# Between the two parts of a fused 8-sequence block: weights of the first local layer loaded into used-up weight memory, statistics taken per batch

## The reference

```python
x = x + L0_attn(layernorm(x), ...)           # piece "a"
x = x + L0_xattn(layernorm(x), ctx, ctx)     # "b", an mLSTM cell
x = x + L0_ffn(layernorm(x), ...)            # "c", 8 experts for each of 4 heads, and an MLP
x = x + L1_attn(layernorm(x), ...)           # "d"
x = x + L1_xattn(layernorm(x), ctx, mask)    # "e"
x = x + L1_ffn(layernorm(x), ...)            # six local layers:
    for i in range(6):
        x = attn_layer(shift_tokens(x), Wqkv[i], q_scale[i], k_scale[i], Wo[i]) + x
        x = ffn_layer(shift_tokens(x), ln_g[i], ln_b[i], W1[i], b1[i], W2[i], b2[i]) + x
```

## Time and profile before

| | us |
|---|---|
| median of 3 runs | 4306.43 |
| lowest and highest | 4299.49, 4312.36 |
| the profiled execution: its own time | 4305.56 |
| the profiled execution: span | 4303.6 |

### The profile page before, as it was taken

How to read it: one execution, slowest core, us unless ns; L and a number is a source line. 1 busy time by engine, 2 the same in 40 slices (tenths; PEclk the granted TensorE clock), 3 DMA queues, 4 the chain that set the end, 5 groups by cost and what they waited for, 6 DMA issues and landing times. The chain is left out here.

```text
span 4303.6 us, 81290 instructions
## 1 busy us (share of the span) xinstructions
PE 3902.0 (91%) x25848; PEld 2840.7 (66%) x25848; DVE 2894.1 (67%) x9138; ACT 2278.2 (53%) x6540; POOL 2268.3 (53%) x2084
## 2 busy tenths in 40 slices
PE   7789989887578999999999999999999999999995
PEld 5667777666346666666666666666666666666664
DVE  4576777655367777767767677766776777777762
ACT  2333333332156666656666666665666566666651
POOL 1565555556175555546556555555655655555540
PEclk8899999988799999999999999999999999999998
DMA  3775565667200000100100001010010001010000
GB/s 116 158 165 139 134 135 135 131 146 158 71 6 11 11 29 19 32 19 9 42 21 27 12 11 38 20 32 9 9 42 18 30 11 41 17 31 11 8 4 25
DMA packets 137427, 224.20 MB, mean 52 GB/s; under 512 B 24656, under 2 KB 98320, under 8 KB 135440
## 3 DMA queue, kind: packets, MB, share of 16 engines
q0 software_dynamic: 40960, 134.25, 14.1%
q1 hardware_dynamic: 96016, 84.41, 6.2%
HBM read 191.39 MB, written 2.10 MB: 45 GB/s over the span
## 5 line engine op out<-in xcount | busy, mean ns | idle before, releaser
L1549 PE MATMUL pj<-l_w_qkv,l_xT 128*128 128x512 f32 x2304 | 1074.1, 603 | 18.6 <-issue 12.6
L1494 POOL TENSOR_TENSOR l_qk_rot<-l_qk_cos,l_qk_sin 128x512 f32<-128x512 f32 x384 | 558.0, 1453 | 411.0 <-DVE l_qk_sin L1814 364.4
L364 POOL DMA_INDIRECT f_rows<-in_emb,f_expert x512 | 514.1, 1004 | 414.1 <-DVE f_expert L1009 227.2
L1549 PEld LDWEIGHTS pj<-l_w_qkv,l_xT 128*128 128x128 f32 x2304 | 418.5, 194 | 404.9 <-issue 389.8
L1629 PE MATMUL pj<-l_xnT,l_w 128*128 128x256 f32 x2112 | 518.8, 391 | 117.9 <-DVE l_hT L1857 108.6
L1709 ACT ACTIVATE l_probs<-l_probs,l_low 128x128 f32<-128x128 f32 x1536 | 593.8, 390 | 2.5 <-DVE l_low L1832 0.7
L1475 POOL TENSOR_TENSOR l_rstd<-l_var_eps,l_minus_half 128x2 f32<-128x2 f32 x48 | 33.4, 696 | 941.8 <-DVE l_var_eps L1788 941.8
L1629 PEld LDWEIGHTS pj<-l_xnT,l_w 128*128 128x128 f32 x2112 | 384.1, 191 | 192.9 <-DVE l_hT L1857 120.0
L1806 DVE TENSOR_REDUCE l_ss<-l_qk_sq 128x8 f32<-128x512 f32 x384 | 261.5, 681 | 366.9 <-ACT l_qk_sq L1696 201.9
L1675 ACT ACTIVATE l_qk_raw<-pj 128x512 f32<-128x512 f32 x384 | 227.3, 592 | 464.7 <-PE pj L1549 450.5
L1832 DVE CUSTOM_DVE_ANT_0 l_probs<-sc,l_shut,l_r_q 128x128 f32<-128x128 f32 x1536 | 437.4, 345 | 51.8 <-PE tp L1588 43.1
(11 more groups left out here) (312 smaller groups left out, 7415.9 us busy)
## 6 DMA issues: line engine op xcount, KB each, us to landing
l_w_qkv<-in_L_ffn_Wqkv SPq DMA_DIRECT2D x12, 1024.0 KB, 6.1
l_w<-in_ff_w SPq DMA_DIRECT2D x6, 1408.0 KB, 6.9
f_rows<-in_emb,f_expert POOLq DMA_INDIRECT x512, 5.8
l_w_qkv<-in_L_ffn_Wqkv SPq DMA_DIRECT2D x12, 512.0 KB, 4.7
l_xs<-l_stream SPq DMA_DIRECT2D x48, 128.0 KB
l_w_o<-in_L_ffn_Wo SPq DMA_DIRECT2D x6, 1024.0 KB, 5.4
l_xf<-l_stream SPq DMA_DIRECT2D x48, 128.0 KB
l_xs<-l_stream SPq DMA_DIRECT2D x48, 127.0 KB
```

Source lines behind the costliest of these rows:

```text
L364: pool.indirect_dma_start(rows[:, j % RH, k, :], None, dram["emb"], bass.IndirectOffsetOnAxis(ap=expert[:, n % 2, at:at + 1], axis=0)).the ...
L1494: pool.tensor_tensor(qk_rot[:, i % ROTS, :], qk_cos[:, b, :], qk_sin[:, b, :], ALU.add).then_inc(rotated if s == 0 else pool_front, 1)
L1549: last = pe.matmul(pj[b][:, :], xT[:, k, t * P:(t + 1) * P], w_qkv[:, k, s * INNER + c * 512:s * INNER + (c + 1) * 512], start=(k == 0), s ...
```

## The change

- `w_qkv` and `w_o` are allocated outside both parts (class `Shared`). In the first part the same memory holds `a_w` (in `w_o`) and `c_wg`, `c_wu`, `c_wd` (in `w_qkv`).
- SyncE, at the end of its order in the first part, waits until `a_y` of the last batch is done and issues the load of `w_o` for layer 0, then waits for the last readers of the three MLP weights and issues those of `w_qkv`. The loads are gone from the start of the second part; `qk_gain` is loaded there as before.
- VectorE takes the entry statistics of a batch (`f_stats`) behind its `e_u`, and POOL the power (`f_rstd`) at the end of its next step. The 16-tile statistics and POOL's power go from the second part.
- VectorE scales one batch at a time, and `entry_done` counts batches. SyncE's `stage_attn` for a batch of layer 0 waits for that batch only.

In `ORDER`, `("f_stats", -5)` is added to "vector" right behind `("e_u", -5)`, ahead of `("c_coef2", -3)`, and `("f_rstd", -6)` to "gpsimd" at the end of its step. The core of the rest:

```diff
-        a_w = sb("a_w", [P, 4, KC, D])
+        a_w = shared.w_o[:, :, :].rearrange("p (w k) d -> p w k d", w=4)
...
-        c_wg, c_wu = sb("c_wg", [P, KC, INTER]), sb("c_wu", [P, KC, INTER])
-        c_wd = sb("c_wd", [P, MC, D])
+        ffn = shared.w_qkv[:, :, :].rearrange("p k n -> p (k n)")
+        c_wg, c_wu = (ffn[:, i * KC * INTER:(i + 1) * KC * INTER].rearrange("p (k n) -> p k n", k=KC) for i in range(2))
+        c_wd = ffn[:, 2 * KC * INTER:2 * KC * INTER + MC * D].rearrange("p (c d) -> p c d", c=MC)
...
+            sp.wait_ge(ps_full, Slot("a_y", BATCH - 1).full)
+            shared.load_o(sp, 0)
+            sp.wait_ge(ps_full, max(Slot(f"c_m{i}", BATCH - 1).full for i in range(MC)))
+            sp.wait_ge(m_used[0], BATCH)
+            sp.wait_ge(m_used[1], BATCH)
+            shared.load_qk(sp, 0)
+            shared.load_v(sp, 0)
...
+            def f_rstd(n):
+                pool.wait_ge(measured, n + 1)
+                pool.tensor_tensor(shared.rstd[:, n, :], shared.var_eps[:, n, :], minus_half[:, 0:TILES], ALU.pow).then_inc(shared.entry_ready, 1)
+
+            do["f_rstd"] = f_rstd
...
+            def f_stats(n):
+                s = Slot("e_u", n)
+                dve.wait_ge(s.taken, s.after)
+                for t in range(TILES):
+                    last = V.bn_stats(f_bn[:, t, :], xall[:, n, t, :])
+                chain.link(last)
+                for t in range(TILES):
+                    last = V.bn_aggr(shared.mv[:, n, t, :], f_bn[:, t, :])
+                chain.link(last)
+                V.tensor_scalar(shared.var_eps[:, n, :], shared.mv[:, n, :, 1], 1e-5, None, ALU.add).then_inc(measured, 1)
+
+            do["f_stats"] = f_stats
...
             def stage_attn(n, row, first):
-                if not first:
+                if first:
+                    sp.wait_ge(entry_done, row + 1)
+                    apart(sp, passed)
+                else:
                     sp.wait_ge(res_f, n - BATCH + 1)
                     apart(sp, passed)
...
-            load_qk(0)
-            load_v(0)
+            load_gain(0)
             sp.wait_ge(consts_set, 2)
-            sp.wait_ge(entry_done, 1)
             stage_attn(0, 0, True)
-            load_o(0)
             load_1(0)
             load_cols(0)
             load_2(0)
...
-                pool.wait_ge(pool_init, 1)
-                pool.wait_ge(entry_stats, 1)
-                pool.tensor_tensor(all_rstd[:, :], all_var[:, :], all_half[:, :], ALU.pow).then_inc(entry_rstd, 1)
...
-                tiles_in = xall[:, :, :, :].rearrange("p b t d -> p (b t) d")
-                tiles_out = stream[:, :, :, :].rearrange("p b t d -> p (b t) d")
-                for i in range(ALLT):
-                    last = nc.vector.bn_stats(all_bn[:, i, :], tiles_in[:, i, :])
-                last.then_inc(dve_entry, 1)
-                dve.wait_ge(dve_entry, 1)
-                for i in range(ALLT):
-                    last = nc.vector.bn_aggr(all_mv[:, i, :], all_bn[:, i, :])
-                last.then_inc(dve_entry, 1)
-                dve.wait_ge(dve_entry, 2)
-                nc.vector.tensor_scalar(all_var[:, :], all_mv[:, :, 1], 1e-5, None, ALU.add).then_inc(entry_stats, 1)
-                dve.wait_ge(entry_rstd, 1)
-                for i in range(ALLT):
-                    last = nc.vector.tensor_scalar(tiles_out[:, i, :], tiles_in[:, i, :], all_mv[:, i, 0:1], all_rstd[:, i:i + 1],
-                                                   ALU.subtract, ALU.mult)
-                last.then_inc(entry_done, 1)
-                dve.wait_ge(entry_done, 1)
+                for row in range(BATCH):
+                    dve.wait_ge(shared.entry_ready, row + 1)
+                    for t in range(TILES):
+                        last = nc.vector.tensor_scalar(stream[:, row, t, :], xall[:, row, t, :], shared.mv[:, row, t, 0:1], shared.rstd[:, row, t:t + 1],
+                                                       ALU.subtract, ALU.mult)
+                    last.then_inc(entry_done, 1)
+                dve.wait_ge(entry_done, BATCH)
...
+    def load_qk(self, sp, l):
+        n = self.w_qkv.shape[2] // 3
+        for k in range(KC):
+            sp.dma_start(self.w_qkv[:, k, 0:2 * n], self.dram["L1_ffn_Wqkv"][l, k * P:(k + 1) * P, 0:2 * n]).then_inc(self.wqk_loaded, 16)
+
+    def load_v(self, sp, l):
+        n = self.w_qkv.shape[2] // 3
+        for k in range(KC):
+            sp.dma_start(self.w_qkv[:, k, 2 * n:3 * n], self.dram["L1_ffn_Wqkv"][l, k * P:(k + 1) * P, 2 * n:3 * n]).then_inc(self.wv_loaded, 16)
+
+    def load_o(self, sp, l):
+        sp.dma_start(self.w_o[:, :, :], self.dram["L1_ffn_Wo"][l].rearrange("(c p) n -> p c n", p=P)).then_inc(self.wo_loaded, 16)
...
+        shared = Shared(w_qkv=sb("w_qkv", [P, KC, 3 * inner]), w_o=sb("w_o", [P, inner // P, D]), mv=sb("entry_mv", [P, BATCH, TILES, 2]),
+                        var_eps=sb("entry_var_eps", [P, BATCH, TILES]), rstd=sb("entry_rstd", [P, BATCH, TILES]),
+                        wqk_loaded=ctx.enter_context(nc.semaphore("wqk_loaded")), wv_loaded=ctx.enter_context(nc.semaphore("wv_loaded")),
+                        wo_loaded=ctx.enter_context(nc.semaphore("wo_loaded")), entry_ready=ctx.enter_context(nc.semaphore("entry_ready")), dram=dram)
```

More of the change, by code:

```diff
@@ L8 @@
 from contextlib import ExitStack
+from dataclasses import dataclass
 import concourse.bass as bass
@@ L39, in apart, with first_layers @@
     eng.sem_inc(passed, 1)
-def first_layers(nc, xall, x_loaded, ident, ident_bf, dram):
+def first_layers(nc, xall, x_loaded, ident, ident_bf, shared, dram):
     H4, DH = 4, 64
@@ L93, in first_layers @@
         ("c_gather5", -4), ("c_gather6", -4), ("c_gather7", -4), ("c_gather8", -4), ("c_gather9", -4), ("c_gather10", -4), ("e_rstd", -5),
+        ("f_rstd", -6),
     ]
@@ L1141, in _, with local_layers @@
             dve.wait_ge(s.taken, s.after)
-def local_layers(nc, xall, ident, ident_bf, passed, dram, layers, out_dram):
+def local_layers(nc, xall, ident, ident_bf, passed, shared, dram, layers, out_dram):
     H, DH = 16, 64
@@ L1211, in sem @@
             return ctx.enter_context(nc.semaphore("l_" + name))
-        w_qkv = sb("w_qkv", [P, KC, 3 * INNER])
-        w_o = sb("w_o", [P, INNER // P, D])
+        w_qkv, w_o = shared.w_qkv, shared.w_o
         w_1 = sb("w_1", [P, KC, TAIL + P])
@@ L1385, in layer @@
                         apart(sp, passed)
-                        load_v(l + 1)
+                        shared.load_v(sp, l + 1)
                     if r == 2 and not first:
@@ L1877, in _, with sb @@
                 nc.vector.tensor_tensor(xall[:, row, :, :], xall[:, row, :, :], stream[:, row, :, :], ALU.add).then_inc(summed, 1)
+@dataclass
+class Shared:
+    w_qkv: object
+    w_o: object
+    mv: object
+    var_eps: object
+    rstd: object
+    wqk_loaded: object
+    wv_loaded: object
+    wo_loaded: object
+    entry_ready: object
+    dram: dict
+    def load_qk(self, sp, l):
[8 more added lines that the diff above has]
+        sp.dma_start(self.w_o[:, :, :], self.dram["L1_ffn_Wo"][l].rearrange("(c p) n -> p c n", p=P)).then_inc(self.wo_loaded, 16)
 def build(nc, dram, out_dram):
     with ExitStack() as ctx:
-        xall = ctx.enter_context(nc.sbuf_tensor("x_all", [P, BATCH, TILES, D], F32))
-        ident = ctx.enter_context(nc.sbuf_tensor("identity", [P, P], F32))
-        ident_bf = ctx.enter_context(nc.sbuf_tensor("identity_bf", [P, P], BF16))
+        def sb(name, shape, dt=F32):
+            return ctx.enter_context(nc.sbuf_tensor(name, shape, dt))
+        xall = sb("x_all", [P, BATCH, TILES, D])
+        ident, ident_bf = sb("identity", [P, P]), sb("identity_bf", [P, P], BF16)
         x_loaded = [ctx.enter_context(nc.semaphore(f"x_loaded{n}")) for n in range(BATCH)]
@@ L1898, in _ @@
                 pool.wait_ge(identity_step, 3)
-        first_layers(nc, xall, x_loaded, ident, ident_bf, dram)
-        local_layers(nc, xall, ident, ident_bf, passed, dram, DEPTH, out_dram)
+        first_layers(nc, xall, x_loaded, ident, ident_bf, shared, dram)
+        local_layers(nc, xall, ident, ident_bf, passed, shared, dram, DEPTH, out_dram)
 def rotary_base():
```

40 lines of the change are left out of this document (15 added, 25 removed), and 8 rows, old and new, of the table ORDER.

## The result

| | median | lowest to highest | runs |
|---|---|---|---|
| before | 4306.65 us | 4299.49 to 4312.36 | 4 |
| after | 4362.41 us | 4357.45 to 4368.72 | 4 |

The ratio is 1.0131, with a 95% interval of 1.0116 to 1.0146. The prediction said 4303 us with a range of 4292 to 4315; it is missed on the slow side, by far more than any of its rivals allowed.

What follows compares the result with a forecast made beforehand. TensorE was busy 91% of the span, the border bound by the chain VectorE, POOL, VectorE, SyncE, DMA. Terms -13.2 + 7 + 3 = -3.2 us on 4305.56 gave 4302.4, predicted as 4303 after 0.9 for the median; range 4292 to 4315.

Steps and rivals of the forecast that it cites:

- its rivals: Four other outcomes: loads find room 4295.3 us (0.2), gathers pay all 4308.5 (0.2), statistics full 4308.9 (0.07), slower stream 4318.2 (0.1).
- From TensorE's first projection to the end nothing changes, 3140 us.: Second part, from TensorE's first projection on: its time stays at 3140 us.
- Term 1, the border: Last add of the first part to first staging DMA: 16.9 us falls to 3.7, a gain of 13.2 us.
- The border costs 0.55 us as now: Between the two parts: VectorE still restarts after 0.55 us.
- the two tiles and the memset: Behind VectorE's restart: scaling two tiles (0.74 us) runs beside the memset of xf (0.96), plus 0.1 for the semaphore.
- The way from staging to TensorE's first work: Start of the second part, first staging DMA to TensorE's first work: stays at 9.7 us.
- Term 2, the loads: End of the first part: 4.2 MB of weight loads beside gathers cost 7 us, between 2.1 and 12.3.
- The slower rival, the mixed stream at the gathers' rate: End of the first part: weights move at 191 GB/s, loads cost 22.0 us, total 4318.2 us; chance 0.1.
- Term 3, the statistics: First part: seven more f_stats and f_rstd on VectorE and POOL cost 3 us, bounds 0 and 8.7.
- The sum: Whole kernel: -13.2 for the border, +7 for loads, +3 for statistics make -3.2 us.

Runs made afterwards that it cites:

- e2: Kernel before with none of the change, but its second part's tensors moved to the changed kernel's addresses; ratio 1.0129 to the kernel before.
- e9: Kernel before with gaps so that xf alone begins 64 bytes past a multiple of 256; ratio 1.0104 to the kernel before.
- e4: e1 with the last batch's power done by POOL at the start of the second part; ratio 0.9982 to the kernel before.
- e15: Changed kernel with a 64-byte gap ahead of xs and the last batch's power moved to the second part; ratio 0.9984 to the kernel before.
- e1: Changed kernel with two unused gaps that put the second part's tensors back at their old places modulo 512 bytes; ratio 1.0011 to the kernel before.
- e13: Kernel before with gaps so that stream begins 128 bytes past a multiple of 256, xs and xf in place modulo 256; ratio 0.9996.
- e14: Kernel before with gaps so that stream begins 64 bytes past a multiple of 256, xs and xf in place modulo 256; ratio 1.0002.
- e16: e15 with SyncE's five weight loads held until the last batch's gathered rows are all added; ratio 0.9965 to the kernel before.
- e5: e4 with SyncE's five weight loads held until the last batch's gathered rows are all added; ratio 0.9983 to the kernel before.
- e6: e1 with statistics, powers and entry norm as in the kernel before, shared memory and early loads kept; ratio 1.0010 to the kernel before.
- e10: Kernel before with a 64-byte gap ahead of stream, moving stream, xs, xf and everything behind up by 64; ratio 1.0161 to the kernel before.

## Why the prediction was wrong, by its own steps

**"From TensorE's first projection to the end nothing changes, 3140 us."** This is the step that failed. It measured +54.1 us. The premise was that no instruction there changes; but removing 704 bytes of one part's tensors moves every tensor behind them, and the staging DMAs of each of 48 steps pay for it; half of the price is TensorE's longer waits, the other half the lower clock behind them. None of the rivals contained such a mechanism. e2 shows it without any of the change, and e9 with one tensor. The Trainium skill has a rule that would have given warning ("DMA: Bandwidth & Descriptors", section "How a descriptor splits into AXI transactions"): a descriptor that doesn't start on a multiple of 256 bytes is fetched from the boundary below and costs extra. The section says this of what is read, and `xf` is written, so it was a hint and no forecast. The runs agree with it only in part. `xf` at 64 costs 27 us of wait, but at 128, where a piece crosses as many boundaries, 2.4; and `stream` on a multiple of 256, by the rule the cheap place, is the dear one.

**Term 1, the border: 3.7 us.** It measured 12.96: 2.06 to the end of the power (2.05 in the sum), 8.20 from there to VectorE's restart (0.55) and 2.70 from there to the staging DMA (1.06). "The border costs 0.55 us as now" failed by 7.65 us, and the two tiles and the memset by 1.64. The 0.55 us were what was left of a barrier whose longest arm, POOL's drain of 8.65 us, was hidden by 31 us of piece e. That row was in the trace of before. The rule of thumb would have been to ask, for an engine that gets a new last instruction, what its queue does behind it. With that arm out of the way (e4, e15) the border is 3.6 us: the 13.2 us of gain were there to be had. That it is the very 3.7 of the sum is luck: in e15 it is made of 1.28 us (no power), 0.36 and 1.95. The way from staging to TensorE's first work was 0.6 us longer (10.26 for 9.68), which the prediction held at nothing. e2 has the same 10.26 without the change and e1 has 9.49, so this too is the addresses.

**Term 2, the loads: +7.** The size is about right, but only one pair of runs bears out the mechanism. The profile shows 5.0 us to the last dots and 6.6 to `c_add`. In the fourth and fifth groups the gathers took 89.0 us with loads beside them (e15) and 79.1, 82.1 and 81.6 without (e13, e14, e16); in the first three 91.0, 92.1, 84.6 and 90.8 against a mean of 87.2 over eight. The pair e15 and e16 gives 8 us, give or take 7. The pair e4 and e5 gave none. The slower rival, the mixed stream at the gathers' rate (22 us), fell with the 227 and 254 GB/s.

**Term 3, the statistics: +3.** Not settled. The five waits of TensorE grew by 2.7 us, where the term had 6.2 as the most and took 3; that fits, but it is one profile against one. In the profile 6.2 us are lost ahead of the first load, but the start of the last batch scatters by more between executions of one first part: in the last two groups it came at 987.8 and 992.6 with the new statistics and at 990.1 and 995.3 without. e6 against e1 says that what they cost in the first part, less the 4.4 us of border that they save, is nothing within some 13 us.

**The sum.** For the change without its two accidents the prediction's terms make -3.2 us, 0.07%; e15 measured 0.16%, with an interval of 0.05 to 0.27. So the loss is 54 us of addresses (e2: 1.29%) and 9 us at the border, most of it drain (e4's border). These make 63, and the medians differ by 55.8: the rest of the change is worth a little, as the terms said. The sum came close with terms of which one is shown (the border), one rests on one pair of runs and one isn't settled, so its nearness to e15 is no proof of each.

## What to carry to other kernels

When a change adds or removes a tensor, write down where the tensors behind it land, and look at the DMAs that read and write them in small pieces on a path that is waited for; an experiment with an unused gap of 64 bytes tells in one run whether a time difference is the edit or the addresses. When a change gives an engine a new last instruction ahead of a barrier, look up in the trace how long that engine's drain is and what has hidden it so far. And price a recurring wait of TensorE by what the clock does behind it as well as by its length: here the wait was half of the loss.

## What the runs showed of the hardware that was not expected

- A staging DMA from SBUF to SBUF in pieces of 512 bytes for each partition: with the target 64 bytes past a multiple of 256, what follows the third DMA's row is 0.5 us longer (3.36 to 3.82) and the row 0.1 us (4.62 to 4.74); with the target at 128 or 0 it isn't (3.41 and 4.63, 3.36 and 4.62). With the source on a multiple of 256 (and 512) the row itself is 0.36 us longer (4.62 to 4.98), with the source at 64, 128 or 192 it isn't (4.66, 4.64, 4.62). With both (e10) the wait grows by 35.8 us, less than the 45.7 of the two alone.
- The drain of POOL's queue at the end of a block took 8.65 us (9.46 in the four runs with the power moved: e4, e5, e15, e16) in the part in which POOL issues 512 gathers, 0.04 us in the small block ahead of it and 0.82 us at the end of the second part, in which it issues none. That the gathers make it long is argued from this alone; it was not tried.
- Idle times of TensorE of 2.7 us instead of 2.1 in each step of a loop brought 45 stretches at the lower clock of 1.2 GHz instead of 30, 61 us more in all; some waits of 2.1 us were followed by one too. The loop loses 27 us of busy time in that way.
